# A vision-transformer block on one core: means from the first norm's scale, dense experts in two batches, centred slot and expert weights

## The reference

```
p = layernorm(patches) * g1 + b1;  y = p @ W_proj          # 768 -> 192
h = layernorm(y) * g2 + b2
q, k, v = split(h @ W_qkv);  q, k normalised over the tokens of an image
attn = softmax(q^T k * temp)                                # 8 heads, 24x24 each
h = layernorm(h + (attn v) @ W_proj + b_proj)
Xn = h / (|h| + 1e-6);  sp = slots / (|slots| + 1e-6) * scale
logits = Xn @ sp                                            # 8 experts x 4 slots
D = softmax over tokens;  C = softmax over slots
H = gelu((D^T Xn) @ W_down + b_down)                        # 192 -> 24, per expert
Y = C @ (H @ W_up + b_up)                                   # 24 -> 192
out = layernorm(h + Y)
```

## Time and profile before

| | us |
|---|---|
| median of three runs (140.8 to 141.6) | 141.26 |
| the profiled execution | 140.0 |
| its span in the trace | 138.0 |
| TensorE, VectorE busy | 115.0, 88.9 |
| ScalarE, GpSimd busy | 69.0, 67.0 |

### The profile page before, as it was taken

The page is one execution under the profiler, slowest core; times in us unless marked ns, Lnnn a source line. Parts: engine busy times, 40 slices in busy tenths (PEclk is TensorE's granted clock), DMA queues, the critical chain, the costliest instruction groups (busy, mean ns, idle before and its releaser), DMA issues.

```text
span 138.0 us, 4819 instructions
## 1 busy us (share of the span) xinstructions
PE 115.0 (83%) x1779; PEld 93.6 (68%) x1779; DVE 88.9 (64%) x380; ACT 69.0 (50%) x234; POOL 67.0 (49%) x158
## 2 busy tenths in 40 slices
PE   0297799999699999999999999997986860999920
PEld 0297799888377868578787796866964630788700
DVE  0211999999643687985857558586987440159980
ACT  3000004242862848648675686846644468763553
POOL 8500277767847428837265382743664000007871
PEclk9999999999999999999999999999999555599995
DMA  1999899988000000000000000000000000000232
GB/s 14 337 293 278 269 305 320 314 319 214 5 7 0 5 0 7 5 0 7 0 5 5 0 5 0 10 5 0 5 0 7 0 0 0 5 0 24 72 89 71
DMA packets 7677, 10.34 MB, mean 75 GB/s; under 512 B 2056, under 2 KB 5032, under 8 KB 7656
## 3 DMA queue, kind: packets, MB, share of 16 engines
q1 hardware_dynamic: 7656, 10.06, 24.2%
HBM read 9.17 MB, written 0.88 MB: 73 GB/s over the span
## 4 chain that ended last, share of the span: by engine, by line
PE 47%; DVE 22%; issue 12%; POOL 10%; ACT 4%; DMA 3%; SPq 1%; POOLq 1%; DVEq 0%; ACTq 0%
DVE st L649 8%; PE ps L565 7%; PE ps L436 6%; PE ps L476 5%; PE ps L496 3%; PE ps L542 3%; PE ps L399 3%; DMA wt<-in_w_tok 3%; PE ps L489 3%; PE ps L519 3%; DVE y L663 3%; PE ps L578 3%; DVE st L671 2%; PE ps L507 2%; PE ps L407 2%
## 5 line engine op out<-in xcount | busy, mean ns | idle before, releaser
L417 PE MATMUL ps<-wc,xT 128*108 128x192 f32 (+1 forms) x132 | 23.0, 327 | 1.5 <-DVE wc L637 1.5
L940 ACT ACTIVATE hT<-ps,b,g 96x108 f32<-96x108 f32 (+1 forms) x22 | 8.4, 430 | 27.9 <-PE ps L426 27.9
L417 PEld LDWEIGHTS ps<-wc,xT 128*108 128x108 f32 (+1 forms) x132 | 20.7, 170 | 2.0 <-DVE wc L637 1.8
L436 PE MATMUL ps<-wqk,hT 96*108 96x384 f32 (+1 forms) x44 | 16.2, 490 | 0.7 <-ACT qp L962 0.7
L1125 POOL TENSOR_SCALAR pw<-mv 108x1 f32<-108x1 f32 (+1 forms) x11 | 3.7, 337 | 21.3 <-DVE mv L780 21.3
L476 PE MATMUL ps<-hT,wv 96*128 96x108 f32 (+1 forms) x88 | 12.5, 284 | 0.0
L1139 POOL TENSOR_SCALAR var<-mv 108x1 f32<-108x1 f32 (+1 forms) x11 | 2.4, 223 | 18.9 <-DVE mv L875 18.4
L950 ACT ACTIVATE sq<-ps 108x384 f32<-108x384 f32 (+1 forms) x11 | 5.4, 490 | 12.4 <-PE ps L436 12.4
L476 PEld LDWEIGHTS ps<-hT,wv 96*128 96x128 f32 x88 | 10.7, 191 | 0.7
L649 DVE BATCH_NORM_STATS2 st<-xs 108x6 f32<-108x384 f32 (+1 forms) x22 | 10.9, 540 | 0.2 <-issue 0.2
L960 ACT ACTIVATE km<-ps,imgsel 108x192 f32<-108x192 f32 (+1 forms) x32 | 11.0, 418 | 0.0
(11 more groups left out here) (106 smaller groups left out, 304.6 us busy)
## 6 DMA issues: line engine op xcount, KB each, us to landing
xT<-in_x_t SPq DMA_DIRECT2D x10, 324.0 KB, 7.0
xs<-in_x SPq DMA_DIRECT2D x10, 324.0 KB
out<-o SPq DMA_DIRECT2D x10, 81.0 KB
wt<-in_w_tok SPq DMA_DIRECT2D x1, 576.0 KB, 4.2
wqk<-in_w_qk SPq DMA_DIRECT2D x1, 288.0 KB, 8.7
xT<-in_x_t SPq DMA_DIRECT2D x1, 216.0 KB, 7.5
xs<-in_x SPq DMA_DIRECT2D x1, 216.0 KB
wv<-in_w_v SPq DMA_DIRECT2D x1, 192.0 KB, 9.0
```

Source lines behind the costliest of these rows:

```text
L417: mm = pe.matmul(tokp(g), xT[:, o + kc * n:o + (kc + 1) * n], wc[:, kc, :], start=kc == 0, stop=kc == KC - 1)
L436: mm = pe.matmul(qkp(g), hT[:, f, t0:t0 + tokens(g)], wqk[:, f, :, :, :].rearrange("p j h d -> p (j h d)"), start=f == 0, stop=f == 1)
L940: ins = act.activation(hT[:, f, t0:t0 + tokens(g)], htp(g)[:, f, :], ACT.Identity, bias=b2[:, f:f + 1], scale=g2[:, f:f + 1])
```

## The change

**Start.** The means are taken from `wt` itself, with the column of g1 / 768 (`gs1`) as weights of the matmul, so `wg` goes. column_means comes first and waits for the weights in two halves; `wc` is made in six scalar_tensor_tensor, and token(0) waits for each piece. offset() comes after token(0), and VectorE's copy of `bw` after x_moments(0). b1 and g1 come in one load; slots and W_down are loaded ahead of x of groups 4 to 10.

**Centred weights.** The third norm's mean is no longer subtracted from the rows that are transposed: `slots` and W_down are centred over their 192 features instead. `feature_means()` on TensorE (step 3) and `centre_weights()` on VectorE (step 3) make that; slot_scale moves from step 4 to 2. turn_z transposes `z` as soon as residual has written it, unit_h1 is gone, the unit length comes into mask_logits and take_d as a factor (`inv3`), and keep_h1 writes the normed rows for last_residual only. GpSimd's ln3_root is one pow of two columns. Logits and all that follow it come one step earlier, and TensorE's loop has 16 steps instead of 17.

**Dense experts.** Two batches of 18 and 14 images. hidden(b) writes whole groups of 32 partitions, gelu is two activations of 128 partitions, `widen(b)` multiplies by W_up in 16 matmuls over row groups of 32, take_lower (ScalarE) and take_upper (VectorE) copy the result, and `turn_u(g)` transposes it for slot_bias. hidden(0) and gelu(0) come in step 11, widen(0) in step 12, and groups 0 to 5 are combined in steps 13 to 16 by the table WIDE.

```diff
-HB = ((0, 4), (4, 8), (8, NG))
+HB = ((0, 6), (6, NG))
...
+HS = 11
+WIDE = {13: (0, 1), 14: (2, 3), 15: (4, 5)}
...
-            sp.dma_start(wt[:, :, :], w_tok.rearrange("(k p) e -> p k e", p=128)).then_inc(wtok_in, 16)
+            sp.dma_start(gb1[:, :, :].rearrange("p t k -> p (t k)"), ln1_gb).then_inc(ln1_in, 16)
+            for i in range(2):
+                k0 = i * KC // 2
+                sp.dma_start(wt[:, k0:k0 + KC // 2, :].rearrange("p k e -> p (k e)"),
+                             w_tok[:, k0 * D:(k0 + KC // 2) * D]).then_inc(wtok_in[i], 16)
...
             sp.dma_start(spraw[:, :, :, :].rearrange("p f n q -> p f (n q)"),
                          slots.rearrange("(f p) n q -> p f (n q)", f=2)).then_inc(slots_in, 16)
             sp.dma_start(scl[:, :], scale.broadcast_to([F, 1])).then_inc(slots_in, 16)
-            sp.dma_start(wd[:, :, :, :].rearrange("p f n h -> p f (n h)"), w_down).then_inc(experts_in, 16)
+            sp.dma_start(wd[:, :, :, :].rearrange("p f n h -> p f (n h)"), w_down).then_inc(wd_in, 16)
+            for g in range(4, NG):
+                load_x(g)
             sp.dma_start(bd[:, :], b_down).then_inc(experts_in, 16)
...
+            def column_means():
+                pe.wait_ge(gs1_ready, 1)
+                for kc in range(KC):
+                    if kc % (KC // 2) == 0:
+                        pe.wait_ge(wtok_in[kc // (KC // 2)], 16)
+                    mm = pe.matmul(csp(), gs1[:, kc:kc + 1].broadcast_to([128, 128]), wt[:, kc, :],
+                                   start=kc == 0, stop=kc == KC - 1)
+                mm.then_inc(csp_ready, 1)
...
-            def column_means():
-                pe.wait_ge(share_set, 1)
-                for kc in range(KC):
-                    pe.wait_ge(wg_ready, kc + 1)
-                    mm = pe.matmul(csp(), share[:, :], wg[:, kc, :], start=kc == 0, stop=kc == KC - 1)
-                mm.then_inc(csp_ready, 1)
...
+            def feature_means():
+                pe.wait_ge(dshare_set, 1)
+                pe.wait_ge(sp_scaled, 1)
+                pe.wait_ge(y1_ready, min(NG, P1 + 1))
+                for f in range(2):
+                    pe.matmul(spmp(), dshare[:, :], spsq[:, f, :, :].rearrange("p n q -> p (n q)"),
+                              start=f == 0, stop=f == 1)
...
+                for f in range(2):
+                    mm = pe.matmul(wdmp(), dshare[:, :], wd[:, f, :, :].rearrange("p n h -> p (n h)"),
+                                   start=f == 0, stop=f == 1)
+                mm.then_inc(wdm_ready, 1)
...
+                    if g == 0:
+                        pe.wait_ge(wc_ready, kc + 1)
                     mm = pe.matmul(tokp(g), xT[:, o + kc * n:o + (kc + 1) * n], wc[:, kc, :],
...
+                if b >= 1:
+                    pe.wait_ge(yt_ready, HB[b][0])
+                    pe.wait_ge(z2_ready, HB[b][0])
+                for e in range(2):
+                    for f in range(2):
+                        for j in range(4):
+                            r = slice(32 * j, 32 * j + 32)
+                            mm = pe.matmul(utp(i1 - i0)[:, j, f, :, e, :], wu[r, e, f * F:(f + 1) * F],
+                                           hb[r, e, 0:(i1 - i0) * NP], start=True, stop=True,
+                                           tile_position=(32 * j, 0))
+                mm.then_inc(utp_ready, 1)
...
+                for f in range(2):
+                    u = widened(b)[:, f, i0:i0 + images(g), :, :]
+                    mm = pe.transpose(ytp(g)[:, f * F:(f + 1) * F],
+                                      u.rearrange("p i j s -> p (i j s)"), ident[0:F, 0:F])
...
-            offset()
             column_means()
-            pe.wait_ge(wc_ready, 1)
             for g in range(P1):
                 token(g)
+                if g == 0:
+                    offset()
...
-            for s in range(17):
+            for s in range(16):
+                if s == 3:
+                    feature_means()
                 at(values, s - 2)
                 at(project, s - 3)
-                at(logits, s - 5)
+                at(logits, s - 4)
...
-                at(turn_xn, s - 4)
-                at(slot_in, s - 6)
+                at(turn_z, s - 3)
+                at(slot_in, s - 5)
...
+                if s == HS:
+                    pe.wait_ge(experts_in, 16 * (2 + 1))
                     hidden(0)
-                if s == NG + 3:
-                    pe.wait_ge(v_ready, NG)
-                    hidden(1)
-            pe.wait_ge(lnn_ready, NG)
-            pe.wait_ge(e2_scaled, NG)
-            slot_out(0)
-            slot_out(1)
-            hidden(2)
-            for g in range(2, NG):
-                slot_out(g)
-                combine(g - 2)
-            combine(NG - 2)
+                if s == HS + 1:
+                    widen(0)
+                for g in wide(s - 1):
+                    combine(g)
+                for g in wide(s):
+                    turn_u(g)
+            hidden(1)
+            combine(4)
+            combine(5)
+            widen(1)
+            turn_u(6)
+            for g in range(7, NG):
+                turn_u(g)
+                combine(g - 1)
             combine(NG - 1)
...
+                dve.wait_ge(ln1_in, 16)
+                dve.tensor_scalar(gs1[:, :], gb1[:, 0, :], 1.0 / PD, None, ALU.mult).then_inc(gs1_ready, 1)
...
+                dve.wait_ge(csp_ready, 1)
                 for kc in range(KC):
-                    dve.tensor_scalar(wg[:, kc, :], wt[:, kc, :], g1[:, kc:kc + 1], None,
-                                      ALU.mult).then_inc(wg_ready, 1)
-                dve.wait_ge(wg_ready, KC)
-                dve.wait_ge(csp_ready, 1)
-                dve.tensor_tensor(wc[:, :, :], wg[:, :, :], csp().unsqueeze(1).broadcast_to([128, KC, D]),
-                                  ALU.subtract).then_inc(wc_ready, 1)
+                    dve.scalar_tensor_tensor(wc[:, kc, :], wt[:, kc, :], gb1[:, 0, kc:kc + 1], csp(),
+                                             ALU.mult, ALU.subtract).then_inc(wc_ready, 1)
...
+                dve.wait_ge(wdm_ready, 1)
+                dve.tensor_tensor(spraw[:, :, :, :].rearrange("p f n q -> p f (n q)"),
+                                  spsq[:, :, :, :].rearrange("p f n q -> p f (n q)"),
+                                  spmp().unsqueeze(1).broadcast_to([F, 2, SL]), ALU.subtract).then_inc(sp_centred, 1)
+                dve.tensor_tensor(wdc[:, :, :, :].rearrange("p f n h -> p f (n h)"),
+                                  wd[:, :, :, :].rearrange("p f n h -> p f (n h)"),
+                                  wdmp().unsqueeze(1).broadcast_to([F, 2, NE * 32]),
+                                  ALU.subtract).then_inc(wdc_ready, 1)
...
+                dve.wait_ge(rt3_ready, g + 1)
+                dve.scalar_tensor_tensor(rt3[0:n, g, 1:2], rt3[0:n, g, 0:1], EPS_L2, rt3[0:n, g, 1:2],
+                                         ALU.mult, ALU.add).then_inc(nrm3_ready, 1)
...
-                dve.reciprocal(inv3[0:n, g:g + 1], nrm3[0:n, g:g + 1]).then_inc(inv3_ready, 1)
-
-            def h1(g):
-                n = tokens(g)
-                dve.wait_ge(r3_ready, g + 1)
-                dve.tensor_scalar(z[0:n, g, :], z[0:n, g, :], mv3[0:n, g, 0:1], r3[0:n, g, 0:1],
+                dve.reciprocal(inv3[0:n, g, :], rt3[0:n, g, :]).then_inc(inv3_ready, 1)
+
+            def keep_h1(g):
+                n = tokens(g)
+                dve.wait_ge(inv3_ready, g + 1)
+                dve.tensor_scalar(h1[0:n, g, :], z[0:n, g, :], mv3[0:n, g, 0:1], inv3[0:n, g, 0:1],
                                   ALU.subtract, ALU.mult).then_inc(h1_ready, 1)
...
-                dve.tensor_scalar(xn[0:n, g, :], z[0:n, g, :], inv3[0:n, g:g + 1], None,
-                                  ALU.mult).then_inc(xn_ready, 1)
...
-                dve.tensor_tensor(lm[0:n, g % NX, 0:s], lgp(g), negmask[0:n, 0:s], ALU.add).then_inc(lm_ready, 1)
+                dve.wait_ge(inv3_ready, g + 1)
+                dve.scalar_tensor_tensor(lm[0:n, g % NX, 0:s], lgp(g), inv3[0:n, g, 1:2], negmask[0:n, 0:s],
+                                         ALU.mult, ALU.add).then_inc(lm_ready, 1)
...
-                dve.tensor_copy(dm[0:n, g % NX, 0:s], dp(g)).then_inc(dm_ready, 1)
+                dve.tensor_scalar(dm[0:n, g % NX, 0:s], dp(g), inv3[0:n, g, 1:2], None, ALU.mult).then_inc(dm_ready, 1)
...
+            def take_upper(b):
...
+                dve.tensor_copy(widened(b)[:, :, :, 2:4, :].rearrange("p f i j s -> p j (f i) s"),
+                                utp(i1 - i0)[:, 2:4, :, :, :, :].rearrange("p j f i e q -> p j (f i) (e q)")).then_inc(uT_upper, 1)
...
+                dve.scalar_tensor_tensor(z2[0:n, g % NQ, :], yop(g), rC[0:n, g:g + 1], h1[0:n, g, :],
...
+            mean_shares()
             token_weights()
             x_stats(0)
             x_moments(0)
+            token_offset()
...
-            for s in range(16):
-                if s == 4:
```

(64 more changed lines are left out.)

220 lines of the change are left out of this document (120 added, 100 removed).

## The result

The kernel after takes 149.26 us (median of 4 runs, 148.67 to 150.64), the kernel before beside it 141.43 (140.80 to 141.62). The ratio is 1.073, 95% interval 1.064 to 1.082. Some executions of a kernel are over 1.5% slower than its fastest, and the ratios leave these out: the two medians alone would give 1.055. I had forecast 139.8 and a range of 137.2 to 143.2. The profiled execution took 150.64, the longest of the four; its span is 148.9 (before: 140.0 and 138.0).

The account below looks back on a forecast made before the run. VectorE bounds the first pass, TensorE the loop, a round of VectorE, ScalarE and GpSimd the late steps. Terms sum to -3.1 at full clock, +1.6 for the clock: -1.5 against 138.0, or 139.8 on the median; range 137.2 to 143.2.

Parts of the forecast that it names:

- The start: Up to the first pass: earlier column_means and x_stats(1) save 1.3 us, bounds -0.5 and -2.3.
- the loads need as long per group as VectorE does within a tenth: First pass: loads of x nearly match VectorE's 2.2 us a group, so its head start holds only if x is there.
- Rival C: Clock falls where it did before (2.7, not 1.6), or loads eat the start's gain (0.8): 140.9 us, chance 0.20.
- The loop to step 11: TensorE's loop up to step 11: 2.4 us of added work less 1.0 hidden, +1.4, bounds +0.4 and +2.4.
- the waits of TensorE in steps 0 to 10 hide 1.0: Loop: TensorE's existing waits, 0.7 + 0.3 us, absorb 1.0 of the 2.4 us of added work.
- Steps 11 and 12: Early hidden(0) and gelu(0) with two table loads make turn_l(8) wait 2.7: 12.4 us against 8.84, +3.6.
- Rival D: Clock falls in step 12's new wait, near 103, doubling TensorE work of steps 12 to 15: 143.6 us, chance 0.18.
- Rival E: The activation table switches drain, as the skill's page says: 142.5 us, chance 0.05.
- Steps 13 to 15: To the end of slot_in(10): one engine round of 4.2 us a step, 10.5 us against 16.0, -5.5.
- From there to the last bn_aggr: After slot_in(10): VectorE sets the pace at 1.38 us a group, 15.0 us against 15.9, -0.9.
- the surcharge of 1.6: Half clock near the end doubles combine, turn_u, hidden(1) and widen: +3.1, 1.5 under VectorE's backlog, so +1.6.
- No return: TensorE's clock falls near 112 and, with thinner work never full again, does not come back.

Follow-up runs that it names:

- e12: The kernel after, unchanged, run again as a second look at its loads: 148.82 us, ratio 1.071.
- e7: The kernel before with the change's new start alone, load order otherwise as before: 144.51 us against 140.62.
- e11: The kernel before with the new start, its weight halves in packets of 768 bytes: 145.73 us, ratio 1.039.
- e17: e7 with VectorE copying the offset row ahead of x_stats(0), so statistics start late: 144.20 us, ratio 1.033.
- e2: The kernel before with only the loads of slots, scale and W_down moved ahead of x(4): 140.55 us against 141.10.
- e3: The kernel after with the token weights in the layout of before and in one load: 147.55 us, ratio 1.048.
- e5: The kernel after with rows of x loaded for groups 0 to 3 alone: 142.75 us, ratio 1.015.
- e1: The kernel after with the loads of slots, scale and W_down put back behind all loads of x: 148.97 us, ratio 1.057.
- e9: The kernel after with the token weights' halves in packets of 768 bytes: 151.82 us against 142.32.
- e10: The kernel before with only the token weights changed, laid out by partition and loaded in two halves of 2304-byte packets: 144.19 us, ratio 1.026.
- e14: The kernel before with six row buffers of x in place of four, removing SyncE's stop: 140.06 us, ratio 1.002.
- e16: The kernel after with the small loads, W_proj, slots and W_down behind x of group 7: 151.40 us, ratio 1.075.
- e6: The kernel before with rows of x loaded for groups 0 to 3 alone: 139.41 us, ratio 1.008.
- e18: The kernel after with the start and load order of before, the rest of the change alone: 144.49 us, ratio 1.037.
- e4: The kernel after with gelu replaced by the identity, so no table switches for it: 145.33 us, ratio 1.037.
- e15: e7 with SyncE waiting ahead of x(4) until the loads of masks and W_proj have landed: 143.57 us against 141.61.
- e13: The kernel after with SyncE waiting ahead of x(4) for masks, W_proj, slots and W_down: 149.73 us, ratio 1.075.

## Why the prediction was wrong, step by step

**The start, -1.3 forecast, +5.4 measured at the first qk.** column_means came at 4.21 (4.5 forecast), and x_stats(1) at 13.59 (13.7 to 14.8), but the latter with luck: in e12, the same kernel, it came at 15.61. The step that failed is "the loads need as long per group as VectorE does within a tenth", and the bound that I drew from it, -0.5 at worst. It took the rate of before for granted, and read even that a little high: the last slice before 34.5 us has 214 GB/s, not 269 to 320. With the new start the rate is a fifth lower (e7, e11, e17: 238 to 254 against 301), a group of 0.66 MB then needs 2.7 us and VectorE 2.2. VectorE waits 8.1 us in all for rows of x, 6.3 of it before groups 3 and 4, with the small loads, slots and W_down between them. The price of the order was mis-sized as well: slots and W_down are 0.17 MB by the profile's page (24 and 144 KB) and not 0.22, and the 0.8 us allowed for them became a wait of 1.6 and 1.9 in e2 and e3, at 273 and 293 GB/s. Rival C had "the loads eat the start's gain" at 0.8 us; it was the right mechanism, but in this profile the loads took 6.7 (from -1.3 to +5.4), in e12's 5.0. e5 shows the start's -1.2 where x is there.

**Why the rate falls stays open.** Each of these alone was tried and is not the cause: the order of the loads (e1, e2), the packets of the weights (e9, e11), their layout and halves without the rest of the start (e10), SyncE's missing stop (e14), the small loads in the middle (e16), VectorE's early statistics (e17). What the kernels with the low rate have in common is the weights in halves together with a column_means that begins on the first half, at 4.1 to 4.7 us; e3, with one load and column_means at 5.6, had the high rate in its profile, and e10, with halves and no early column_means, had it too. But the same kernels also have the halves right behind one load of gain and offset. e3 has that one load and no halves, e10 the halves behind two loads; so the sequence of the first loads is a rival to the early column_means, and no run tells the two apart. The tiles' places in memory differ too and were not tried by themselves. The rate is low from early on, not only in the first pass: between 5 and 18 us it is 247 after and 288 before. What the loads cost, 4.5 us by the medians, rests on the pair e5 and e6 and not on the cause.

**The loop to step 11, +1.4 forecast.** It is +4.3 in the kernel after and in e18 (33.89 to 97.03), both with 3.4 us at half clock early in the loop (from 43.2 and from 38.3), and +2.6 in e5, +3.2 in e12, which have none. So that fall is not part of the change: the kernel after has it in one profile and not in the other, and e6 has it in the kernel before and takes 60.1 us there for 58.8: 1.3. The 2.4 of added work was a little low (2.6 to 3.2). The step that failed is "the waits of TensorE in steps 0 to 10 hide 1.0": none of it was hidden, since the added work stands in steps 3 to 5 and the waits in steps 0 and 1. Of the 4.3 in the kernel after, some 1.2 go with the clock (63.1 against 62.0 in e12).

**Steps 11 and 12, 12.4 forecast, 14.0 measured** (102.81 to 116.80; 8.84 before). The wait of turn_l(8), its place and its cause were right: 2.7 forecast, 2.23 measured. Too small was step 11 itself, 6.4 us to the end of hidden(0) where I had 5.2: hidden(0) takes 1.53, and turn_l(7) waits 0.72 for its mask_logits. From there turn_l(8) came after 4.6 us (5.0 forecast), and the rest took 3.1 (2.2), since the clock falls to half at 114.9, which makes widen(0) 1.57; project behind it takes 1.55. I had put that fall at 112 but charged it to combine, turn_u and hidden(1) alone. e4 shows the price of the early gelu: 4.6 us from hidden(0) to slot_in(10), 2.0 for the wait and 2.6 for the clock behind it. Rival D (the clock falls behind the new wait) named this, with its time of 143.6. Rival E falls: the table load takes 1.28 us and the next activation follows at once (109.32, 110.61; 111.17, 112.46), as in the earlier trace rows; the cost came from who waited. The Trainium skill (ScalarE: Activation LUTs, What ACT_TABLE_LOAD costs) puts a switch at 2.66 us, of which 1.28 are the load and 1.38 a drain. This trace agrees on the load and shows no drain.

**Steps 13 to 15, 10.5 forecast at the full clock, 12.0 measured** (116.80 to 128.79). e4, mostly at the full clock, needs 10.2 (113.25 to 123.42). The sum of the step was right, the clock was not in it.

**From there to the last bn_aggr, 15.0 forecast, 16.1 measured**, all at half clock; with the surcharge of 1.6 it was right. VectorE's groups follow at 1.2 to 1.25 us, where I had 1.38. **Last bn_aggr to the end:** 4.0, as forecast (4.4 less 0.4).

**The clock.** "No return" was half right: before, it was half for 13.7 us; now it falls at 114.9, comes back for 3.4 us at 118.3, and is half from 121.7 to the end, 27 us. In the first 47 us it is half in two more places, 6.8 us from 26.2, after TensorE had stood nearly idle from 22 to 25 us, and 3.4 us from 43.2.

So of the 10.9 us between these two spans, some 5.4 stand at the first qk, 4.3 in the loop and 1.2 at the end. The 4 us by which steps 13 to 15 became shorter went to the longer steps 11 and 12 (+5.2) in front of them. And the loads are not the whole miss: e18, the change without its start and at 290 GB/s, still costs 4.9 us (ratio 1.037), where the forecast of these parts was -0.2.

## What to carry to other kernels

Where two rates agree within a tenth, moving the start of one side is first of all a test of the other: take the loads away once (as e5 did) and see what the start is worth, before costing it. A rate read off a trace belongs to that program; here a change at the front moved it by a fifth for the next 25 us. An activation function that needs another table was cheap by itself (1.3 us each way) and dear where other engines waited for ScalarE's next exponential; the gap of 2 us that it made cost as much again in TensorE's clock (2.6 us, e4). A fall of the clock in one profile may be that execution's: profile a kernel twice before the fall is charged to a change (e12).

## What the runs showed of the hardware

The rate of identical loads behind an identical order differs by a fifth between programs that differ only in the first few microseconds (e7 with 248, the kernel before with 301), at nearly the same busy share of the DMA engines, 0.90 and 0.92. In one execution it came back behind a stop in which the queue ran empty (e15: 62, then 319 GB/s), in another it did not (e13: 101, then 276 and 256).

TensorE's clock fell to half for 3.4 us early in the loop in some executions and not in others of the same kernel (the kernel after from 43.2; e12 not). Behind a gap of 2.2 us it fell within 2.0 us (113.73 and 114.9; 107.96 and 110.0 in e18); without the gap (e4) it stayed full for 9.6 us behind the same instruction.
